# A two-layer gated block on one core: normalising and routing moved out of stages of their own

## What is computed

```python
x = x + tanh(g_xattn[0]) * L0_xattn(layernorm(x), ctx, ...)   # 16 heads of 128, self and cross
x = x + tanh(g_ffn[0])   * L0_ffn(layernorm(x), ...)
x = x + tanh(g_xattn[1]) * L1_xattn(layernorm(x), ctx, ctx, mask, Wq, Wk, Wv, Wo)
x = x + tanh(g_ffn[1])   * L1_ffn(layernorm(x), ...)

# L0_ffn: 16 experts of width 176, 4 per row, and a shared expert of width 704
probs = softmax(x @ gate_w.T); topk_w, idx = top_k(probs, 4); topk_w /= topk_w.sum(-1)
shared = silu(x @ sg.T) * (x @ su.T) @ shared_down.T * sigmoid(x @ shared_gate_vec.T)
out = shared + sum over e of combine[:, e] * silu_mul(x @ gate_up[e].T) @ down[e].T

# L1_xattn: 16 query heads of 16, 4 key and value heads, alibi bias, mask, softmax, @ Wo

# L1_ffn: 8 experts of width 176, 2 per row, and a shared one of width 176
scores = sigmoid(x @ gate_w.T); top 2, divided by their sum, times 2.5
out = sum over e of combine[:, e] * (silu(x @ w1[e]) * (x @ w3[e])) @ w2[e] + shared
```

## Time and profile before

| | us |
|---|---|
| runs shown (three): lowest, median, highest | 1698.15, 1698.78, 1702.68 |
| the profiled execution's own time | 1697.2 |
| its span, from the first to the last instruction | 1695.4 |
| PE busy | 1500.9 (89%) |
| DVE busy | 1270.9 (75%) |
| ACT busy | 1033.5 (61%) |
| POOL busy | 824.3 (49%) |

### The profile page before, as it was taken

The page is one execution under the profiler, slowest core; times in us unless marked ns, Lnnn a source line. Parts: engine busy times, 40 slices in busy tenths (PEclk is TensorE's granted clock), DMA queues, the critical chain, the costliest instruction groups (busy, mean ns, idle before and its releaser), DMA issues. The chain is left out here.

```text
span 1695.4 us, 40055 instructions
## 1 busy us (share of the span) xinstructions
PE 1500.9 (89%) x11666; PEld 1162.7 (69%) x11666; DVE 1270.9 (75%) x4601; ACT 1033.5 (61%) x3244; POOL 824.3 (49%) x1254
## 2 busy tenths in 40 slices
PE   0589999999999999999768879997799997799998
PEld 0489888988889888989644447775566665355554
DVE  5589999999999999999768556664688884544454
ACT  4578888788888888778543435554477774222222
POOL 0766666666666666666314754443566661000000
PEclk9999999999999999999969989999899997799999
DMA  7594300000000000000023634442422200000000
GB/s 299 158 224 109 69 0 0 0 0 0 0 0 0 0 0 0 0 0 1 1 83 100 211 119 122 127 122 89 139 61 72 67 28 3 1 13 1 12 12 12
DMA packets 75227, 95.59 MB, mean 56 GB/s; under 512 B 32138, under 2 KB 60298, under 8 KB 73606
## 3 DMA queue, kind: packets, MB, share of 16 engines
q1 hardware_dynamic: 68278, 75.53, 15.7%
q0 software_dynamic: 6864, 19.01, 3.1%
HBM read 62.74 MB, written 40.43 MB: 61 GB/s over the span
## 5 line engine op out<-in xcount | busy, mean ns | idle before, releaser
L665 ACT ACTIVATE prob<-bS,ntop 128x128 f32<-128x128 f32 x512 | 186.2, 419 | 4.6 <-DVE ntop L474 4.4
L569 POOL TENSOR_TENSOR rs<-ve,half 128x6 f32<-128x6 f32 x128 | 176.8, 1381 | 0.0
L649 ACT COPY pT<-bP 128x512 f32<-128x512 f32 x128 | 75.6, 591 | 144.8 <-PE bP L331 144.8
L577 POOL TENSOR_SCALAR kv<-kv,rs,nb 128x128 f32<-128x128 f32 x256 | 150.4, 593 | 27.5 <-POOL nb L572 27.3
L451 DVE SCALAR_TENSOR_TENSOR qn<-qn,mv,rs 128x128 f32<-128x128 f32 x512 | 155.7, 364 | 6.6 <-POOL rs L569 5.1
L322 PE MATMUL bS<-kT,qT 128*128 128x128 f32 x1024 | 138.2, 278 | 10.8 <-ACT prob L665 10.8
L298 PE MATMUL bq<-w,xq 128*128 128x256 f16 x1024 | 135.0, 276 | 6.6 <-DVE xq L423 6.6
L636 ACT ACTIVATE qT<-bqT,vecs 128x256 f32<-128x256 f32 x256 | 134.6, 594 | 2.5 <-PE bqT L282 2.4
L322 PEld LDWEIGHTS bS<-kT,qT 128*128 128x128 f32 x1024 | 126.0, 194 | 14.0 <-issue 12.7
L339 PE MATMUL bO<-pT,kv 128*128 128x256 f32 x512 | 132.4, 381 | 1.6 <-ACT pT L649 1.6
L356 PE MATMUL bY<-wproj,catq 128*128 128x256 f16 x1024 | 132.7, 273 | 0.8 <-DVE catq L494 0.8
(11 more groups left out here) (296 smaller groups left out, 4307.7 us busy)
## 6 DMA issues: line engine op xcount, KB each, us to landing
f_xblk<-by_slot SPq DMA_DIRECT2D x79, 132.0 KB, 2.1
by_slot<-zeros SPq DMA_DIRECT2D x1, 10112.0 KB, 36.5
l_back<-by_pick SPq DMA_DIRECT2D x16, 512.0 KB, 3.5
f_wstage<-by_expert SPq DMA_DIRECT2D x16, 480.0 KB
l_piece<-in_f_w SPq DMA_DIRECT2D x16, 312.0 KB, 2.9
wo_stage<-in_wproj SPq DMA_DIRECT2D x8, 512.0 KB, 4.2
by_expert<-in_f_w SPq DMA_DIRECT2D x18, 128.0 KB, 2.8
x<-in_x SPq DMA_DIRECT2D x1, 2048.0 KB, 8.5
```

The costliest lines, as they stand in the source:

```text
L569: nc.gpsimd.tensor_tensor(rs[:, t, :], ve[:], r["half"][:, 0:6], ALU.pow).then_inc(rs_ready, 1)
L577: done = nc.gpsimd.tensor_scalar(key, key, rs[:, t, 4 + j:5 + j], nb[:, t, j:j + 1], ALU.mult, ALU.add)
L665: done = nc.scalar.activation(prob[:, t, h, :], bS[:, h, :], ACT.Exp, bias=ntop[:, t, h:h + 1], accum_out=total[:, t, h:h + 1])
```

## The change

Four things are done, all of the same computation.

1. The gate's weight of the first feed-forward is split with the first attention's weights. `normalise` is gone. The first normalising, the logits and the split of the six shared tiles of 768 columns now stand inside `sparse_ffn`'s block: even batches are normalised on ACT, odd ones on DVE, in pairs; shared tiles 0 and 1 are split during the last pairs and tiles 2 to 5 at steps n = 0 to 3. POOL takes the power in two parts, of 4 and 12 batches.
2. The second attention's small weights, wo and alibi are loaded by SP behind the fifth routed block's load and split during blocks 16 to 23, into the memory of the shared tiles (`common`).
3. The second feed-forward's normalising and routing is a class, `ChunkRouter`, that works on one chunk of four batches. Chunk 0 is routed in the last steps of `attention1`; chunk c+1 is routed inside chunk c of `feed_forward`.
4. `feed_forward` is one loop over 52 tiles, with no emptying at a chunk's end; `f_bw` is one bank instead of two, and the other bank, `bx`, serves the router.

The diff, cut to its core:

```diff
@@ sparse_ffn: SP @@
+            for j in range(NS):
+                reach(sp, s["tile_low"], j - len(tile_stage) + 1)
+                sp.dma_start(tile_stage[j % len(tile_stage)], shared_in[:, j * TILE_W:(j + 1) * TILE_W]
+                             ).then_inc(tile_loaded[j % len(tile_stage)], 16)
             sp.wait_ge(r["prepared"], r["prepared_all"])
             sp.wait_ge(s["cleared"], 2)
+            sp.wait_ge(s["tile_low"], NS)
...
                 sp.dma_start(xblk[:, i % FETCH, :], by_slot[i * P:(i + 1) * P, :]).then_inc(x_loaded[i % FETCH], 16)
+                if i == FETCH:
+                    sp.wait_ge(s["downed"], STEPS)
+                    sp.wait_ge(s["w_low"], E)
+                    for j, (src, _, _) in enumerate(small):
+                        sp.dma_start(small_stage(j), src).then_inc(s["small_loaded"], 16)
+                    for into, src in later:
+                        sp.dma_start(into, src).then_inc(s["later_loaded"], 16)
@@ sparse_ffn: PE @@
+            def turn_pair(p):
+                reach(pe, s["logits_taken"], p - 1)
+                pe.wait_ge(s["even_normed"], p + 1)
+                pe.wait_ge(s["odd_normed"], p + 1)
...
             def up(n):
                 c, j, t = n // NS, n % NS, n % 2
+                if c == 0:
+                    pe.wait_ge(s["tile_low"], j + 1)
...
+            turn_pair(0)
+            for p in range(PAIRS):
+                if p + 1 < PAIRS:
+                    turn_pair(p + 1)
+                project_pair(p)
@@ sparse_ffn: ACT @@
+            norm_even(0)
+            norm_even(1)
+            for p in range(PAIRS):
+                take_pair_high(p)
+                if p + 2 < PAIRS:
+                    norm_even(p + 2)
+                if p >= 1:
+                    take_pair_logits(p - 1)
+                if p in (PAIRS - 4, PAIRS - 2):
+                    split_tile_high((p - PAIRS + 4) // 2)
+            take_pair_logits(PAIRS - 1)
+
             for n in range(STEPS + 1):
+                if n < NS - AHEAD:
+                    split_tile_high(n + AHEAD)
...
+                for j, (_, high_part, _) in enumerate(small):
+                    if i == 4 * FETCH + 2 * j:
+                        act.wait_ge(s["small_loaded"], 16 * len(small))
+                        nc.scalar.activation(high_part, small_stage(j), ACT.Copy, scale=WS).then_inc(s["small_high"], 1)
@@ sparse_ffn: DVE (the low halves stand as ACT's high ones do), POOL @@
+            for i, part in enumerate((slice(0, CH), slice(CH, B))):
+                nc.gpsimd.tensor_tensor(rs[:, part], rs[:, part], r["half"][:, part], ALU.pow).then_inc(s["rs_r"], 1)
+                pool.wait_ge(s["rs_r"], i + 1)
+                nc.gpsimd.tensor_tensor(nb[:, part], nb[:, part], rs[:, part], ALU.mult).then_inc(s["nb_r"], 1)
@@ ChunkRouter: PE's parts @@
+    def pe_turn(self, pe, c, p, bank):
+        reach(pe, self.s["low"], 2 * c + p)
+        reach(pe, self.s["shares_r"], c)
+        pe.wait_ge(self.s["normed"], 2 * c + p + 1)
+        into = bank.rearrange("p (k j s) -> p k j s", k=KT, j=2)
+        for j in range(2):
+            for k in range(KT):
+                done = self.nc.tensor.transpose(into[:, k, j, :], self.xn[:, j, k * P:(k + 1) * P], self.r["ident"])
+        done.then_inc(self.s["turned"], 1)
...
+    def pe_logits(self, pe, c, bank):
...
+        for i in range(CH):
+            for j, (k, a, w) in enumerate(terms):
+                done = self.nc.tensor.matmul(bank[:, i * NL:(i + 1) * NL], xT[a][:, k, c * CH + i, :], gw[w][:, k, :],
+                                             start=(j == 0), stop=(j == len(terms) - 1))
@@ feed_forward: PE, ACT, DVE @@
+                reach(pe, hid_done, n)
+                if j == 0:
+                    pe.wait_ge(router.s["shares_r"], c + 1)
...
+            for n in range(N):
+                c, j = divmod(n, NT)
+                up(n)
+                if n >= 2:
+                    down_tile(n - 2)
+                if c + 1 < NC:
+                    if j in (2, 4):
+                        router.pe_turn(pe, c + 1, j // 2 - 1, bx[:])
+                    if j == 6:
+                        router.pe_logits(pe, c + 1, bx[:])
+                    if j == 11:
+                        router.pe_shares(pe, c + 1, bx[:])
...
+                    if j in (3, 5):
+                        router.act_high(act, c + 1, j // 2 - 1, bx[:])
+                    if j == 7:
+                        router.act_logits(act, c + 1, bx[:])
...
+                if j == 1 and c > 0:
+                    add_result(c - 1)
+                if c + 1 < NC:
+                    if j == 1:
+                        router.dve_norm(dve, c + 1, 0)
+                    if j == 3:
+                        router.dve_low(dve, c + 1, 0, bx[:])
+                        router.dve_norm(dve, c + 1, 1)
+                    if j == 5:
+                        router.dve_low(dve, c + 1, 1, bx[:])
+                    if j == 8:
+                        router.dve_scores(dve, c + 1)
+                    if j == 9:
+                        router.dve_shares(dve, c + 1)
+                    if j == 10:
+                        router.dve_parts(dve, c + 1)
+                    if j == 12:
+                        router.dve_take_shares(dve, c + 1, bx[:])
@@ attention1: PE @@
+                if at_end(b, B - 2, c, 3):
+                    pe.wait_ge(x_low, B)
+                    router.pe_turn(pe, 0, 0, bx[:])
+                if at_end(b, B - 1, c, 1):
+                    router.pe_turn(pe, 0, 1, bx[:])
+                if at_end(b, B - 1, c, 3):
+                    router.pe_logits(pe, 0, bx[:])
+                if at_end(b, B, c, 2):
+                    router.pe_shares(pe, 0, bx[:])
-
-            pe.wait_ge(small_low, len(small))
```

More of the change, by code:

```diff
@@ L1398, in feed_forward @@
+def feed_forward(nc, r, tag, NT, router, gu, down, gate, out):
+    x, xT, cwT, sel = r["x"], r["xT"], router.q["cwT"], router.q["sel"]
+    SHARED = router.q["shared"]
+    N = NC * NT
     with ExitStack() as ctx:
@@ L1498, in _ @@
+        @block.gpsimd
+        def _(pool):
+            router.pool_scales(pool, rest, 1)
         @block.vector
@@ L2243, in _layout @@
+            attention1(nc, r, t["f1_w"], weights[0], t["mask"], by_pick, shares0, router)
+            feed_forward(nc, r, "f1", NT1, router, weights[1], weights[2], 3, out)
 def _layout(i):
```

747 lines of the change are left out of this document (345 added, 402 removed).

## The result

| | us |
|---|---|
| four runs of the changed kernel | 1665.35, 1675.75, 1683.46, 1687.49; median 1679.61 |
| the kernel before beside them | 1698.15 to 1702.68; median 1698.51 |
| ratio of the two | 0.9862, 95% interval 0.9826 to 0.9899 |
| the profiled execution's own time and span | 1665.35, 1663.6 |

The change makes the kernel faster by 1.0 to 1.7% in this measurement. I had forecast 1664.5 us, a ratio of 0.980, and a range to 1676. The plain median lies 15 above the forecast, outside the range; the ratio applied to the median before gives 1675. The four runs spread over 22 us, and the profiled one is the shortest. Two later measurements of the same code gave 1668.4 (1666.6 to 1668.7, ratio 0.9799, interval 0.9769 to 0.9829) and 1665.3 (1663.4 to 1670.1, ratio 0.9816, interval 0.9794 to 0.9839).

What follows compares the result with a forecast made beforehand. TensorE was taken as the bound in most stages, chains of small steps over several engines in two short stretches. Terms +0.2 −2.6 +1 −8.1 +1.5 −32.1 −3.2 +9 = −34.3 gave a median of 1664.5 us, range 1655 to 1676.

Steps and rivals of the forecast that it cites:

- The second normalising, −32.1: Between second attention's last statistics and first feed-forward matmul: the stretch goes whole except the barrier, −32.1 us (−31 to −32.5).
- First stage, −2.6: First normalising and shared experts in one block: 5.3 us gained, 2.7 lost to weight splits, −2.6 (−6 to +1).
- Small loads, +1: Routed blocks: the small weights' loads behind block load 4 may make load 5 a little late, +1 us (0 to +4).
- Head, −8.1: Second attention's head: small loads and splits leave, first score at 1206.5 instead of 1214.65, −8.1 us (−9.7 to −5.5).
- 1186.6 + 19.1: Second attention's head: projections start at 1186.6, the old 19.1 us to first score stays, giving 1205.7, taken as 1206.5.
- Tail, +1.5: Second attention's last two and a half batches: chunk 0's router work, TensorE part about 2.8 us, partly covered, +1.5 (0 to +4).
- Router, +9: Second feed-forward: router work on TensorE costs 3.0 us a chunk, three times, nothing hiding it, +9 (6 to 12).
- No drains, −3.2: Second feed-forward: three waits of 1.05 us at chunk ends go, the last stays, −3.2 (−2 to −4).
- the slower rival: Feed-forward: each of 24 router steps makes TensorE wait a round trip, at worst about +60 us, 1759; chance 0.03.
- the one of 0.5 us per step: Smaller-gain rival, feed-forward: each of 24 router steps pauses TensorE 0.5 us, +12, 1676 us; chance 0.13.
- The larger gain: Rival: tile splits hidden (−2.7), load 5 on time (−1), a third of router work falls into waits (−3): 1657.5 us; chance 0.14.
- the last one: Rival, first stage: no gain, scatter starts 2 us later, not 2.6 earlier, +4.6, 1669 us; inside the sum's region, chance 0.69.

Runs made afterwards that it cites:

- logit bank run: Changed kernel with a pair's logits in a bank of their own in the first normalising; 1661.1 us, ratio 0.9781 to the kernel before.
- the mean of nine: Nine traces with the small loads behind block load 4, as in the changed kernel; routed blocks mean 177.9 us, against 176.1 before the change.
- the runs with the loads elsewhere: Four traces of edited changed kernels, small loads at the second attention's head or spread over the routed blocks; routed blocks 175.8 to 176.2 us.
- the run without it: Changed kernel with chunk 0's routing moved from the second attention's last steps to the feed-forward's front; 1676.8 us against 1668.4.
- without the router the part: Changed kernel without the routing of chunks 1 to 3 in the second feed-forward, all using chunk 0's rows and shares; 1659.4 us against 1668.4.

## Why the prediction was right, and where not

- **The second normalising, −32.1:** −32.08. The read of the earlier trace rows was all there was to it. That the same work costs little elsewhere was the real question, and there two of my prices were off, in opposite directions.
- **First stage, −2.6:** −2.63, by the mechanism given, but its two parts are each off and cancel. The first scale's power took 1.04, a pair 2.38, a tile's low half 0.95 and its high half 0.84, and the first shared matmul stood at 869.42 (forecast 869.4). Counted from attention 0's last statistics that matmul is 6.0 earlier, not 5.3, and the way from it to the first scatter is 3.3 longer, not 2.7 (35.86 against 32.52): four low halves of 0.95 stand in DVE's row there, and little of them was hidden. The logit bank run shows that the pair chain sets the first part; no run takes the splits out of the second. The bound of the earlier trace rows held: the scatter's end starts the routed blocks.
- **Small loads, +1:** +1.6 in the trace, 1.8 in the mean of nine. Block load 5 took 6.6 us, and TensorE waited 0.39 for it at 1011.90; the runs with the loads elsewhere have all of the stage's 1.8 back. The load did not run independently of the megabyte but landed just behind it. That fits what the prediction cites from the Trainium skill (DMA: Bandwidth & Descriptors, section Two DMAs through the same engine are not ordered): descriptors of one queue start in order. Its user was late by less than the load, since loads run up to four blocks ahead of it.
- **Head, −8.1:** −5.9. The failed step is "1186.6 + 19.1", which took the old length from first projection to first score. That length is 22.5 in the changed kernel, 3.4 more, of which the forecast had allowed 0.8. Two terms were missing. The first three projections run at the lower clock, 1.57 to 1.60 apart instead of 0.85; before two did, 1.60 and 1.38 apart, so this is +1.0. The other +2.5 is waiting for DVE: TensorE waits 1.01 and 1.53 for values and longer for the normalised rows, because three picks in a row stood beside POOL's mask and key blocks and took 0.97, 2.00 and 1.98 us instead of 0.48. Before, one pick of 2.01 did, with one wait of 1.20. I had named this (−5.5 "if the new DVE order makes them wait more") and chosen a value near the other end; the trace of the kernel before had the row that prices it, shown below.
- **Tail, +1.5:** +3.45 over before, 4.7 by the run without it. The failed step is that "the last batches' score work is thinning out and covers part of it". Of the 3.45, 2.1 lie between the first score and the last mask matmul; half of that is there without the router too (200.5 against 199.5 before), for a reason that no run shows. The other 1.4 lie in the drain: there the chain through the engines is the time, TensorE is busy 8.1 of 10 us, at a clock of 0.53, and nothing covered the added steps.
- **Router, +9:** +5.6 to 5.7. The term was mis-sized, 1.9 a chunk instead of 3.0. The eight transposes lengthened their tiles by 0.88 in all instead of 1.32, the 24 matmuls of 8 columns by 0.61 where I had 0.5 to 1.04 (priced in part from a row at the lower clock), the shares' turning by 0.42 instead of 0.47. The rest of the 3.0 was for changes of data type, which no row shows.
- **No drains, −3.2:** the three waits (1.05, 0.99 and 0.99) are gone. 5.7 − 3.0 = +2.7 against +2.47 seen; without the router the part is 3.1 shorter than before.
- **Rivals:** no step made TensorE wait in the feed-forward, so the slower rival and the one of 0.5 us per step are both refuted by the tile periods. The larger gain had its conditions wrong as well: the splits were not hidden and load 5 was not on time. The scatter starts 2.0 us earlier in the span, not 2 later, which refutes the last one.

Two errors of −3.3 (router) and +4.2 (head and tail together) nearly cancel, which is luck; the sum of the trace is −31.8 against −34.3. The sign and the size were right because one term is 32 of it. That the first measurement's ratio stays inside the range is thin: its plain median lies outside, for a cause that no trace shows.

## What to carry to other kernels

A stage that is a chain of small steps over several engines is worth taking apart into the neighbours' loops: 32 us went, and what came back was 1.9 a chunk for three chunks in a loop bound by TensorE and at most 4.7 for one chunk in a thinning tail. Price work in a drain by its whole chain and not by TensorE's share of it; in the open at the loop's front the same chunk cost 13.9. A shorter head is worth only what the first loop step does not give back: of 3.4 us gained to the first score 1.0 were left one batch on. Before pricing a DVE instruction with two inputs in SBUF, look at what POOL runs beside it.

## What the runs showed of the hardware

DVE's pick (two inputs of 128x256 in SBUF) takes 0.48 us alone and 2.00 beside POOL's key block. First a pick and the wait behind it from the kernel before, then a single pick and the key blocks beside it in the changed kernel's head:

```profile
1199.53 2.01 DVE L1834 SCALAR_TENSOR_TENSOR x<-l_back,shares,x 128x256 f32<-128x256 f32 x1
...
1202.25 0.35 PE L1667 MATMUL l_bP<-wv,ctx 128*128 128x64 f16 x6 [1.20 <-DVE l_vv L1806]
```

```profile
1192.61 2.00 DVE L1875 SCALAR_TENSOR_TENSOR x<-l_back,shares,x 128x256 f32<-128x256 f32 x1
```

```profile
1192.38 3.98 POOL L1986 TENSOR_TENSOR l_kblock<-l_kt,headmask 128x1024 f32<-128x1024 f32 x2
...
1194.80 0.35 PE L1701 MATMUL l_bP<-common,ctx 128*128 128x64 f16 x6 [1.01 <-DVE l_vv L1847]
...
1197.35 0.35 PE L1701 MATMUL l_bP<-common,ctx 128*128 128x64 f16 x6 [1.53 <-DVE l_vv L1847]
```

The pick starts 0.23 after the first of two key blocks of some 1.9 and ends 0.3 after it. All 18 lengthened picks of this trace, from 0.67 to 2.00 us, end 0.27 to 0.28 after the end of the POOL instruction that they met, and so do the 16 of the kernel before: a pick waits for that end and does not run at half speed. The Trainium skill has this as a rule (SBUF — State Buffer, section SBUF: two separate sides): an instruction of DVE with two SBUF inputs and one of GpSimd that reads SBUF take a shared pair of ports in turn, each for its whole length. The trace agrees, here with up to 1.5 us a pick, and moving POOL's blocks away brought 0.48 back.
